# Four mixture-of-experts outputs instead of three scaled on ScalarE and summed on GpSimd, with a copy and a scale moved too

## What is computed

```
x = x + attention(LN(x), ctx)        # 16 heads of 8, q and k RMS-normalised
x = x + ffn(LN(x))                   # int8-like quantised, a 3-tap convolution, SiLU
x = x + gated(LN(x), ctx):           # one head of 128
    bf = LN(x) @ w1.T + b1;  p = softmax(bf @ ctx.T / sqrt(128))
    out = [LN(x), p @ ctx] @ w2.T + b2
x = x + moe(LN(x)):                  # 8 experts of width 256, top_k with k = 128
    out = sum over e of affinity_e * ((silu(x Wg_e) * (x Wu_e)) @ Wd_e)
```

## Time and profile before

| | |
|---|---|
| median of 3 runs | 1244.02 us (1242.15 to 1244.71) |
| the profiled execution's own time | 1241.23 us |
| its span | 1239.2 us |
| busy: PE / DVE / ACT / POOL | 1100.0 (89%) / 991.8 (80%) / 825.6 (67%) / 680.8 (55%) |
| mean granted TensorE clock | 0.939 |

### The profile page before, as it was taken

How to read it: one execution, slowest core, us unless ns; L and a number is a source line. 1 busy time by engine, 2 the same in 40 slices (tenths; PEclk the granted TensorE clock), 3 DMA queues, 4 the chain that set the end, 5 groups by cost and what they waited for, 6 DMA issues and landing times.

```text
span 1239.2 us, 27099 instructions
## 1 busy us (share of the span) xinstructions
PE 1100.0 (89%) x9701; PEld 775.9 (63%) x9701; DVE 991.8 (80%) x2728; ACT 825.6 (67%) x1685; POOL 680.8 (55%) x827
## 2 busy tenths in 40 slices
PE   1466667998989899999989999999999999989998
PEld 1333435676757667676767676776767676667775
DVE  3567676988979898988989898989889897877653
ACT  1144455786858677786868676877868686867655
POOL 3202131757474755757574756657574747365775
PEclk9556577999999999999999999999999999999999
DMA  6120212131221303131211212121312212011000
GB/s 204 30 53 20 45 28 61 29 60 31 42 47 34 63 19 61 37 60 30 47 47 38 56 35 51 32 61 37 60 31 46 44 26 56 18 26 25 19 10 9
DMA packets 151395, 53.62 MB, mean 43 GB/s; under 512 B 116832, under 2 KB 150624, under 8 KB 150880
## 3 DMA queue, kind: packets, MB, share of 16 engines
q1 hardware_dynamic: 149248, 47.82, 18.0%
q10 hardware_dynamic: 2016, 4.08, 0.9%
HBM read 24.73 MB, written 4.19 MB: 23 GB/s over the span
## 4 chain that ended last, share of the span: by engine, by line
PE 74%; DVE 11%; SPq 5%; POOL 3%; ACT 3%; issue 2%; DMA 1%; POOLq 0%; DVEq 0%; ACTq 0%
PE py L743 15%; PE pa L594 5%; PE pa L561 4%; SPq L437 4%; PE pg L733 4%; PE pu L733 3%; PE pg L735 3%; PE pg L734 3%; PE pu L735 3%; PE pu L734 3%; PE pa L584 3%; PE pb L641 2%; PE pa L601 2%; DVE q_st L1144 2%; PE pa L743 2%
## 5 line engine op out<-in xcount | busy, mean ns | idle before, releaser
L951 POOL TENSOR_TENSOR moe<-moe 128x512 f32<-128x512 f32 x256 | 335.9, 1316 | 295.4 <-ACT moe L886 149.4
L743 PE MATMUL py<-wd_s,moe 128*128 128x128 f32 x1856 | 249.4, 279 | 3.2 <-POOL moe L951 3.1
L743 PEld LDWEIGHTS py<-wd_s,moe 128*128 128x128 f32 x1856 | 232.4, 192 | 20.5 <-issue 7.8
L872 ACT ACTIVATE tg<-pg 128x512 f32<-128x512 f32 x232 | 139.5, 601 | 105.7 <-PE pg L735 105.0
L1144 DVE TENSOR_REDUCE q_st<-pa 128x4 f16<-128x480 f32 x256 | 168.1, 657 | 37.8 <-PE pa L561 37.2
L1296 DVE SCALAR_TENSOR_TENSOR moe<-tg,pg 128x512 f32<-128x512 f32 x232 | 157.0, 677 | 31.8 <-ACT tg L872 29.7
L886 ACT ACTIVATE moe<-pu 128x512 f32<-128x512 f32 x232 | 140.2, 604 | 33.7 <-PE pu L735 31.7
L806 ACT ACTIVATE probs<-pa 120x512 f32<-120x512 f32 x256 | 139.7, 606 | 25.0 <-PE pa L584 24.6
L561 PE MATMUL pa<-kbd,qht 128*128 128x480 f16 x256 | 102.1, 399 | 34.5 <-DVE q_st L1144 32.1
L733 PE MATMUL pg<-x4h,wg_h 128*128 128x512 f16 x232 | 88.9, 383 | 16.5 <-DVE moe L1296 16.4
L910 POOL TENSOR_SCALAR xn<-x,lnm,lnr 128x128 f32<-128x128 f32 x192 | 87.0, 465 | 5.2
(11 more groups left out here) (196 smaller groups left out, 2535.8 us busy)
## 6 DMA issues: line engine op xcount, KB each, us to landing
kbd<-kht SPq DMA_DIRECT2D x512, 3.8 KB
xin<-in_x SPq DMA_DIRECT2D x16, 256.0 KB, 2.8
xres<-in_x SPq DMA_DIRECT2D x16, 256.0 KB, 3.0
out_x<-acc SPq DMA_DIRECT2D x16, 256.0 KB, 3.2
ctxt_a<-in_ctx_t SPq DMA_DIRECT2D x16, 240.0 KB, 2.7
ctxt_b<-in_ctx_t SPq DMA_DIRECT2D x16, 240.0 KB, 3.0
ctxn_b<-in_ctx SPq DMA_DIRECT2D x16, 240.0 KB, 3.7
wd_s<-in_wd ACTq DMA_DIRECT2D x1, 1024.0 KB, 10.0
```

The costliest lines, as they stand in the source:

```text
L743: mm = pe.matmul(moe_y(g, e)[:, j, :], hu[:, u % 3, j * S:(j + 1) * S], wd_s[:, u, :], start=(half == 0 and j == 0), stop=(half == 1), ski ...
L872: act.activation(tg[:, u % 2, :], moe_bank("g", g, u)[:, :], ACT.Tanh, scale=0.5 / WSCALE).then_inc(tg_done.sem, 1)
L951: pool.tensor_tensor(hu[:, u % 3, :], gw[:, u % 3, :], us[:, u % 3, :], ALU.mult)\
```

## The change

Experts 1, 3, 5 and 6 go by way of ACT and POOL in place of 2, 4 and 6; DVE keeps 0, 2, 4 and 7. The copy of q into q_hi goes from DVE to ACT, as a step of ACT's own queue, and what follows on DVE becomes a step of its own (low). The factor 1/sqrt(128) of the gated scores goes into bft (with the bias scaled once, in aw1c_s), so that the maximum needs no scaling on DVE. All strings of TURNS but the shortest are new. The core of the diff:

```diff
-SIDE = (2, 4, 6)
+SIDE = (1, 3, 5, 6)
...
-                 "s1": ["s1", "nmax"], "p1n": ["rl", "p1n"], "gate": [("gate", i) for i in range(5)]}
+                 "rms_q": ["rms_q", "low"], "p1n": ["rl", "p1n"], "gate": [("gate", i) for i in range(5)]}
...
+                elif step == "rms_q":
+                    act.wait_ge(qf_done.sem, qf_done.at(g))
+                    if later(g):
+                        act.wait_ge(qht_in.sem, qht_in.at(g - 1, 16))
+                    act.activation(q_hi[:, :, :], qb[:, :, :], ACT.Copy).then_inc(q_hi_done.sem, 1)
...
-                    act.activation(bft[:, :], pd[:, :], ACT.Identity, bias=aw1b_s[:, 0:1]).then_inc(bf_done.sem, 1)
+                    act.wait_ge(b1_done.sem, 1)
+                    act.activation(bft[:, :], pd[:, :], ACT.Identity, bias=aw1c_s[:, 0:1], scale=D ** -0.5).then_inc(bf_done.sem, 1)
...
-                    if nth(e) == 3:
-                        act.wait_ge(sum_done.sem, sum_done.at(g, 1))
+                    if nth(e) >= 3:
+                        act.wait_ge(sum_done.sem, sum_done.at(g, nth(e) - 2))
...
-                    cn.link(dve.tensor_tensor(q3, q3, rq, ALU.mult))
-                    if later(g):
-                        dve.wait_ge(qht_in.sem, qht_in.at(g - 1, 16))
-                    dve.tensor_copy(q_hi[:, :, :], qb[:, :, :]).then_inc(q_hi_done.sem, 1)
+                    dve.tensor_tensor(q3, q3, rq, ALU.mult).then_inc(qf_done.sem, 1)
+                elif name == "low":
...
-                    cd.mark(dve.tensor_reduce(nmax1[:, :], pd[:, 0:GB * SC].rearrange("p (t k) -> p t k", t=GB), AX.X,
-                                              ALU.max, negate=True))
-                elif name == "nmax":
-                    cd.meet()
-                    dve.tensor_scalar(nmax1[:, :], nmax1[:, :], D ** -0.5, None, ALU.mult).then_inc(nmax1_done.sem, 1)
+                    dve.tensor_reduce(nmax1[:, :], pd[:, 0:GB * SC].rearrange("p (t k) -> p t k", t=GB), AX.X,
+                                      ALU.max, negate=True).then_inc(nmax1_done.sem, 1)
```

More of the change, by code:

```diff
@@ L45 @@
 WSCALE = 64.0
-LINKS_N, LINKS_A, LINKS_B, LINKS_D = 13, 4, 18, 7
+LINKS_N, LINKS_A, LINKS_B, LINKS_D = 12, 4, 18, 6
 S0, S1, BM, BO, PB = range(5)
@@ L67 @@
         "n": "nnnnnnn",
[L68 to L76, removed]
+        "wna": "wnwnanaaaawaaaaaaaannaaaaaaaaaaaaaanaaaaaaaaaaaawwnaaa",
+        "nab": "aaaabaaabbnaaabaabbbbnanbabaaabbaaabaabanabbaaabbnaaababaabbanbaaaaabnaaa",
+        "nabd": "baaanddbbdabaaaabaababanbdbbbaadanbaababdbaaabaadabaaaaabnaanabbbadnadabbnaaaadadaba",
+        "nabdc": ("cbbaccacacacadcaccabdcacacanbdcababdnabcaccbdanbccacbcacabcabcbabcndnaccaccaabbcbacdcaaccaacbabc"
+                  "caancbdacadacabccabacaccdacbcdabccan"),
+        "abdc": ("cabbcaccacdacacacacacbdacbdaadbbcbaccaacacbcaadcbccbaaaccbacbacdacccbbdacccbabcbacacaaacbadcacaa"
+                 "bbadcaccbaacbccaccdcbacadbcac"),
+        "bdc": "cbbcccccccdbcdcbdccdbbdcbccccbbcccccbcbdbcbcbdbcccbcbccbcccbcbdccbccbccdbccccdccdcb",
+        "dc": "ccccdcccccccccccccdccdccdcccccccdcdccdccccdcccccdcccdccdccc",
         "c": "cccccccccccccccccccccccccccccccccccccccccccccccc",
@@ L80 @@
         "n": "nnnnnnn",
[L81 to L89, removed]
+        "wna": "nawwnanaawaaaaaaaaaaanaaaawaaaanaaaanaaaaaaawaaaaaaana",
+        "nab": "aaabaabaabanaabbbnbaabanbabaaabbaaaabaabbaabnaababaaaaabnabbabnbaaabanaaa",
+        "nabd": "dbaaadbbadbnaabaaaabnaaabbdbaabbnbaaabdaabnbdaaadanabanbaadbaaaaadabbababbaaadnaaabd",
+        "nabdc": ("ccbabccacaacacacdcabdcaabcdacnaababncdcbcbcaanbbccacccaacacbdabacbabbcacdacccadcacbnaccnbdabaaaa"
+                  "cnacacbbccabcacacbabadcdccncabccdaca"),
+        "abdc": ("aacbbaccaccacaccdcaaabadbcdaacbbcdccdacbaaccaabbccacabacbaaccabbcdcccdabccbccaabacacabacbbaacaca"
+                 "aadccbacaccbdbcbadcacccbcdaac"),
+        "bdc": "bdbcccccccbcdccbdbccbddbccccbbccccbbdbcbbcccdccbccbcccbcbccbcccbbcccdccbccbdbcdcccd",
+        "dc": "ccccccccccccdcccccdccdcccccdccdccdcccdccccdcccdccccdcccdccc",
         "c": "cccccccccccccccccccccccccccccccccccccccccccccccc",
@@ L92 @@
     "dve": {
[L93 to L105, removed]
+        "n": "nnnnnnnnnnnnnnnnnn",
+        "wna": "wnwnnannwanaaaaaaannanaanaananaannnanaaaaaaaaaaaaanaanaaaaaawaawaaaaa",
+        "nab": ("abbaanabbaabbbanbbaaabbaabanbbnbnabnaaaabananbabaanbaanbaaabbnnbaabnnbbaanbbbabbaababbnaaaaanaaa"
+                "bbaan"),
+        "nabd": ("bbddaadbnbbbbabnabbbaaaadaaabnbdabbadaabndnnnadaanbbnabnnbaannaannaababbanaabnbbaabbaaabbdbbadaa"
+                 "daabndbbdabaaaadbdaaddd"),
+        "nabdc": ("bbccadaccabdbaaccbbbacaccnaabcnabaddnbcabcbdacbcdbcdnacncbndcabcncandbcaacncaaaanncbcbabcccabcac"
+                  "nananbccbaanbccabaababcnanccbbbbadncbccdcaadbaaababaccbadacacdcdbddcdca"),
+        "abdc": ("abccbacdcacdabcbbbbccaadcbaabcbadaaccdbcaacaacabcbacbccaacbbddbcaacacacbcbaccacbccbbabaccababdbc"
+                 "aabacdaadcadaccacbaabbdbccabbbbbcccaaaadccdddbadcacdc"),
+        "bdc": ("bbcdccdcdbcbbccbcbbbcdbcbbcdcbbcdccccbdcbccdbccbbbcccbcbbbcbcccccbbcbbcbdccdcbbddccbccbbccccbddc"
+                "cddcdbd"),
+        "dc": "cccccccdcdcccccdccccdcccdccccccddccdccccdcccccdddcccccdcccdddddccc",
         "c": "cccccccccccccccccccccccccccccccccccccccccccccccc",
@@ L772, in do_w @@
                     act.activation(gate_h[:, :], gate_f[:, :], ACT.Copy, scale=WSCALE).then_inc(gate_hi.sem, 1)
+                    act.activation(aw1c_s[:, :], aw1b_s[:, :], ACT.Copy, scale=D ** -0.5).then_inc(b1_done.sem, 1)
                 elif step == "wg":
@@ L852, in do_d @@
                         ins = act.activation(p1[:, j, :], pd[:, j * SC:(j + 1) * SC], ACT.Exp, bias=nmax1[:, j:j + 1],
-                                             scale=D ** -0.5, accum_out=l1[:, j:j + 1])
+                                             accum_out=l1[:, j:j + 1])
                     ins.then_inc(p1_done.sem, 1)
```

45 lines of the change are left out of this document (23 added, 22 removed).

## The result

| | before | after |
|---|---|---|
| median | 1243.8 us (1242.15 to 1244.71, 4 runs) | 1255.26 us (1254.05 to 1255.57, 4 runs) |
| profiled execution, its span | 1241.23, 1239.2 us | 1254.05, 1251.7 us |
| start of proj in body 3 (end of the fill) | 214.24 us | 207.91 us |
| from there to proj of body 15 (twelve periods) | 823.67 us | 838.90 us |
| from there to the end | 201.29 us | 204.89 us |

The ratio is 1.01, 95% interval 1.0084 to 1.0117: slower by 1%, clear of noise. The profiled execution's own time grew by 12.8 us. Its span grew by 12.5 us, and the three stretches share it out as -6.3 (fill), +15.2 (twelve periods, 1.27 each) and +3.6 (drain). The mark is the first matmul of proj, which closes every body.

A forecast was written before the change was run, and what follows sets the result against it. PE's own work was taken to bound a period (65.39 of 68.00 us busy). 12 x (0.5 + 0.25) - 1 + 0.6 = +8.6 us on 1241.23 gave 1249.8, plus 2.8 for the median 1252.6 us, range 1237 to 1266.

The forecast's parts named there:

- The ring: Loop h2t3, maximum, hr, hq, hit3, kbd DMAs, max0.3, closing once a period; forecast to take 0.15 to 0.65 us more, 0.5 taken.
- the collision: DVE's quant4, delayed, meets POOL's hu of units 1 and 2, so PE's xit waits; 0 to 1.2 us, 0.25 taken.
- one of 0.2 near scores3.0: PE wait of 0.2 us because stacks3 has only u13 before scores3.0; not added to the sum.
- ACT's 0.6: Counting ACT's queue from stacks3's copy on, hq ends near 895.9, 0.6 us later than before.
- The head (4): Period's head: 1.32 us before g1 stays, max0.2's wait falls to about 0.5, kbd's landing gates max0.3; 0.5 us most gain.
- The q copy (2): Copy of q's high half: DVE loses 0.43 us, ACT takes 0.65; neither end moves the sum.
- Totals (1): Busy sums a period: DVE 58.1, ACT 52.9, POOL 43.4 us, all under PE's 65.4; expert move gives POOL 1.27.
- Fill: Start of the kernel: DVE sheds 0.6 us a group; -1 us over four groups, with -5 to +5 allowed.
- Drain: End of the kernel: d11's add between POOL's hu of 13 and 14; +0.6 us, bounds 0 and 1.3.
- A: Rival, faster: the ring gets shorter, 12 x -0.5 = -6 us, with -3 of the fill 1235 us; chance 0.24.
- B: Rival, no change: the ring as long as before, only fill and drain differ, within 2.5 us, 1244; chance 0.17.
- C: Rival, much slower: the collision in each period at 1.2 us plus other PE waits, +24 us, 1268; chance 0.14.

The follow-up runs named there:

- e7: Changed kernel with three kbd DMAs ahead of hit3, and on PE d4, d5 and d9 parted from the scores ahead of them: 1250.78 us, ratio 1.0065.
- e11: Changed kernel with h2t3 put back ahead of g14 and scores3.1 on PE alone, ACT's order kept: 1254.03 us, ratio 1.0088 against the kernel before.
- e4: Changed kernel with expert 5 back on DVE, experts 1, 3 and 6 on ACT and POOL: 1262.44 us, ratio 1.0156 against the kernel before.
- e2: Changed kernel with three of the sixteen kbd DMAs moved ahead of hit3 on SP: 1246.95 us, ratio 1.0037 against the kernel before.
- e6: Changed kernel with the copy of q's high half back on DVE: 1278.06 us, ratio 1.0289 against the kernel before.
- e8: Kernel before with three kbd DMAs ahead of hit3, the changed kernel's four fill strings and the old DVE step: 1241.99 us, ratio 0.9987.

## Why the prediction was right, point by point

The forecast of 1252.6 us and its side, slower, held: 1255.26. By its sum:

- **The twelve periods: 9.0 forecast, 15.2 measured.** The ring was to cost 0.5 and the collision 0.25 a period. Over the eleven intervals from 277.8 us on, the waits for kbd in the table of waits come to 9.3 us, less those of before (0.23, 0.60, 0.18, 0.38) 7.9; the shorter wait for max0.2 gives back 0.64 each, of which g2's own wait for gw of unit 1 takes 0.29. That leaves 7.9/11 - 0.35 = 0.37 us. xit's wait rose from 3.6 to 6.3 us, 0.25 each. The first term was 0.13 too high, the second right in this trace. About 0.5 us more a period is what the sum left out, and it is the third row of the table above. 0.30 of it are three short waits of PE, at stacks3, scores3.0 and scores3.1. The prediction did announce one of 0.2 near scores3.0 and did not add it, as lying inside ACT's 0.6; it measured 0.10 and was paid beside the ring, with two more like it. The other 0.20 is PE's own time, taken as unchanged because the same matmuls run. It isn't the same time when the groups stand in another order (0.10 for a d behind scores is shown by e7).
- **The head (4).** The 1.32 us stayed, max0.2's wait fell, to 0.33 where I said about 0.5, and kbd gated max0.3. Right.
- **The ring (5).** Each sign named ahead is there: the wait for kbd, ACT full from stacks3 on. In an undisturbed period hq is 0.22 us later against proj, in the range 0.15 to 0.65. That ACT's queue sets it, which I used to choose the value, is shown by e11 (PE alone changes nothing) and e4 (without expert 5's copies hq is 0.57 us earlier), and that the wait for kbd and the disturbed periods hang on SP's queue behind hit3 is shown by e2.
- **The collision (6).** L1194 is at 2.14 to 3.05 us in nine of eleven periods and PE's xit waits in eight by the list. The term 0.25 came out, but by luck: quant4 takes 1.09 us at 10.28 after proj, 0.92 at 10.53, 2.14 at 10.66 and 10.71, and 0.92 at 10.81.
- **The q copy (2).** "Neither end moves the sum" holds only for the new order with the copy on ACT, which is the case that was forecast. Taken back in that order it costs 1.76 us a period (e6). I had priced the copy (on ACT it took 0.63 us, and I took 0.65), and not what it pushes into POOL's way.
- **Totals (1).** ACT's 52.49 and POOL's 43.51 us a period are near the forecast 52.9 and 43.4. DVE's is 60.45, not 58.1: quant4 has 1.05 of it back, and three other DVE groups 0.52, at the same work. Most of the remaining 0.8 is less overlap: the lengths of DVE's instructions added up fall by 0.19 us, while the time in which any of them runs grows by 0.34.
- **Fill: -1 forecast, -6.3 measured**, outside the bound of -5. I gave the split of rms_q no term of its own, and e8 shows that without the moved parts the new strings gain nothing. **Drain: +0.6 forecast, +3.6 measured.** The 2.9 us wait for POOL's hu fell to 2.1, but g1's wait of 1.17, kbd's 0.7 in the body before and new waits for POOL's hu at L744 came in. Against the periods' +6.2 stand -5.3 and +3.0 here, so the span is 3.9 us off (12.5 against 8.6), and the total 2.7, since the execution's own time grew by 0.3 more than the span and the median lies only 1.2 us above the profiled execution and not 2.8. That the total is so near owes something to misses that cancel.

Of the rivals, A (the ring gets shorter) is out by the 0.22 us, B by the periods. C's mechanism, the collision in each period with its full price, was there in four of eleven periods of after (2.8 us or more for quant4); those periods are 70.8 to 71.05 us long, so C described the disturbed ones.
